# Prologue of a two-layer expert kernel: order of two loads, idle products among the logits, and who normalises the rows

## The reference, cut to what matters

```python
x = x + 0.5 * ffn(layernorm(x), Wg, W11, W12, W2)
x = x + attn(layernorm(x), ...)
x = x + 0.5 * ffn(layernorm(x), Wg, W11, W12, W2)

def ffn(x, Wg, W11, W12, W2):          # 8 experts, 2 chosen per row
    scores, idx = top_k(softmax(x @ Wg), 2)
    scores = scores / (scores.sum() + 1e-8)
    gate, value = x @ W11[e], x @ W12[e]          # 256 -> 512
    return sum over the two e of scores[e] * ((gate * sigmoid(gate) * value) @ W2[e])
```

## Time and profile before

| | us |
|---|---|
| median of 3 runs | 987.4 |
| lowest and highest | 986.29, 987.94 |
| the profiled execution, its own time | 985.32 |
| its span | 983.5 |
| busy in the span: PE, DVE, ACT, POOL | 903.3, 582.7, 391.2, 575.8 |
| mean granted clock, as a share of 2.4 GHz | 0.962 |

### The profile page before, as it was taken

One profiled execution on the slowest core, in us unless ns is written; L12 is line 12 of the kernel. 1 busy time (PEld: TensorE's weight loads), 2 busy tenths in 40 slices (PEclk: granted clock), 3 DMA queues, 4 the chain that ended last, 5 costly groups with the idle time before them and its releaser, 6 DMA issues.

```text
span 983.5 us, 19046 instructions
## 1 busy us (share of the span) xinstructions
PE 903.3 (92%) x5396; PEld 778.3 (79%) x5399; DVE 582.7 (59%) x1394; ACT 391.2 (40%) x768; POOL 575.8 (59%) x605
## 2 busy tenths in 40 slices
PE   7769999999999999949897996899999999999994
PEld 6658888888888888827775874688888888888883
DVE  3986565675665655556726887555555555555551
ACT  3644244343443433325443775133333333333331
POOL 3435565666666665357514651577777777777762
PEclk9979999999999999968999996899999999999997
DMA  9654525526336281086202555654433333333332
GB/s 313 204 179 138 205 69 189 185 75 205 131 126 203 94 267 56 28 267 193 65 1 85 162 179 176 214 139 77 78 55 75 54 74 75 53 75 53 54 46 25
DMA packets 83936, 121.50 MB, mean 124 GB/s; under 512 B 12944, under 2 KB 62736, under 8 KB 83888
## 3 DMA queue, kind: packets, MB, share of 16 engines
q1 hardware_dynamic: 45376, 57.88, 18.1%
q0 software_dynamic: 24992, 37.32, 17.5%
q10 hardware_dynamic: 13520, 25.70, 7.7%
HBM read 73.62 MB, written 47.25 MB: 123 GB/s over the span
## 4 chain that ended last, share of the span: by engine, by line
PE 76%; DVE 7%; DMA 5%; ACT 5%; POOL 3%; issue 3%; ACTq 1%; SPq 0%; POOLq 0%
PE bank L1456 40%; PE bank L1479 20%; PE bank L1465 6%; PE bank L1448 3%; PE bank L1577 3%; ACT work L879 1%; DMA seq<-xt 1%; PE bank L1635 1%; DMA seq<-x_rows 1%; PE bank L1625 1%; ACT work L812 1%; ACT work L870 1%; DMA out_rows<-yb,idx_i 1%; PE bank L1394 1%; DMA seq<-y_rows 1%
## 5 line engine op out<-in xcount | busy, mean ns | idle before, releaser
L1165 DVE TENSOR_TENSOR sg<-sg,bank 128x512 f32<-128x512 f32 x142 | 97.7, 688 | 282.7 <-ACT sg L741 282.7
L1456 PE MATMUL bank<-w_hi,xt_hi 128*128 x568 | 237.8, 419 | 4.5 <-DVE xt_lo L1154 4.4
L1456 PE MATMUL bank<-w_hi,xt_lo 128*128 x568 | 225.1, 396 | 0.0
L1456 PE MATMUL bank<-w_lo,xt_hi 128*128 x568 | 225.0, 396 | 0.0
L733 ACT ACTIVATE yb<-bank,gates_in 128x256 f32<-128x256 f32 x142 | 67.3, 474 | 313.8 <-PE bank L1479 276.0
L551 POOL DMA_INDIRECT xg<-xn_rows,idx_i x142 | 140.1, 987 | 72.6 <-issue 41.4
L555 POOL DMA_INDIRECT gates_in<-gate_rows,idx_g x142 | 136.2, 959 | 48.0 <-issue 42.7
L1479 PE MATMUL bank<-w_hi,ft_hi 128*128 x568 | 160.3, 282 | 2.2 <-ACT yb L733 2.2
L1479 PE MATMUL bank<-w_lo,ft_hi 128*128 x568 | 160.5, 283 | 0.0
L1479 PE MATMUL bank<-w_hi,ft_lo 128*128 x568 | 160.4, 282 | 0.0
L565 POOL DMA_INDIRECT out_rows<-yb,idx_i x71 | 114.9, 1619 | 63.2 <-ACT yb L733 53.4
(11 more groups left out here) (289 smaller groups left out, 1293.8 us busy)
## 6 DMA issues: line engine op xcount, KB each, us to landing
w_lo<-w_lo_rows SPq DMA_DIRECT2D x32, 512.0 KB, 4.6
w_lo_rows<-w_lo ACTq DMA_DIRECT2D x16, 512.0 KB
xn_rows<-work SPq DMA_DIRECT2D x14, 512.0 KB, 3.4
seq<-y_rows SPq DMA_DIRECT2D x10, 512.0 KB, 5.2
x_all<-x SPq DMA_DIRECT2D x8, 512.0 KB, 9.0
w_lo_rows<-in_sb ACTq DMA_DIRECT2D x16, 256.0 KB, 2.4
gate<-x SPq DMA_DIRECT2D x16, 256.0 KB, 5.8
seq<-w ACTq DMA_DIRECT2D x7, 512.0 KB, 4.5
```

What stands on the lines that cost most here:

```text
L1165: nc.vector.tensor_tensor(sg[p], sg[p], ps_g[p][:], ALU.mult).then_inc(f_step, 1)
L1456: last = nc.tensor.matmul(dst[p][:], xt[p][:, c, :], of(w), start=(c == 0 and n == 0), stop=(c == DC - 1 and n == len(parts) - 1))
```

## The change

Four things, all in the prologue.

- SyncE asks for five parts of `xt` first, and then for x and the rest of `xt` in turn.
- TensorE gets eight idle products ahead of the loop over the chunks, and four ahead of each chunk's logits. They write bank 3, which `fold` uses later.
- `apply_x` leaves VectorE. GpSimd does it for chunks 0, 2, 4 and 6, each behind that chunk's `rsqrt_x`, with the same waits, that for the zero rows among them.
- ScalarE does it for chunks 1, 3, 5 and 7: three after the variances of chunks 2, 4 and 6, the last where `apply_x(7)` was. The waits of SyncE, ScalarE and VectorE for these rows follow (`norm_dve` becomes `norm_pool`).

```diff
--- before.py
+++ after.py
@@ -270,7 +270,7 @@
         xn_x_out = [sem(f"xn_x_out{b}") for b in range(3)]
         y_in = [sem(f"y_in{b}") for b in range(3)]
         y_out = [sem(f"y_out{b}") for b in range(2)]
-        x_early, x_late, half_sum, summed, norm_dve, norm_act, r_ready = (sem(n) for n in ("x_early", "x_late", "half_sum", "summed", "norm_dve", "norm_act", "r_ready"))
+        x_early, x_late, half_sum, summed, norm_pool, norm_act, r_ready = (sem(n) for n in ("x_early", "x_late", "half_sum", "summed", "norm_pool", "norm_act", "r_ready"))
         x_in = [sem(f"x_in{b}") for b in range(4)]
         x_out = [sem(f"x_out{b}") for b in range(4)]
         xn_out = [sem(f"xn_out{b}") for b in range(2)]
@@ -317,9 +317,11 @@
                 sp.dma_start(x_all[:, k * G:(k + 1) * G, :], rows(x, k)).then_inc(x_all_in[k], 16)
 
             sp.dma_start(wg_sb[:, :, 0:E], wg.rearrange("(c p) e -> p c e", p=P)).then_inc(s_wg, 16)
-            for k in range(NCH):
-                sp.dma_start(xt_raw[0][:, k * CH:(k + 1) * CH], xt[0:P, k * CH:(k + 1) * CH]).then_inc(xt_in[k], 16)
-                load_x(k)
+            for k in range(NCH + 4):
+                if k < NCH:
+                    sp.dma_start(xt_raw[0][:, k * CH:(k + 1) * CH], xt[0:P, k * CH:(k + 1) * CH]).then_inc(xt_in[k], 16)
+                if k >= 4:
+                    load_x(k - 4)
             sp.dma_start(pw_sb, pw.rearrange("(c p) d -> p c d", p=P)).then_inc(s_setw, 16)
             sp.dma_start(wint_sb, wint.rearrange("(c p) n -> p c n", p=P)).then_inc(s_setw, 16)
             sp.dma_start(woutt_sb, woutt).then_inc(s_setw, 16)
@@ -333,10 +335,7 @@
                     e = expert_of_slot(sp, 0)
                     load_up(sp, 0, e)
                     load_down(sp, e)
-                if k < NCH // 2:
-                    sp.wait_ge(norm_dve, k + 1)
-                else:
-                    sp.wait_ge(norm_act, k + 1 - NCH // 2)
+                sp.wait_ge(norm_act if k % 2 else norm_pool, k // 2 + 1)
                 sp.dma_start(rows(xn_dram, k), xn_x[k % 3]).then_inc(xn_x_out[k % 3], 16)
 
             def store_gates(r):
@@ -593,8 +592,21 @@
                 for t in range(ET - 3, ET):
                     scatter(t)
 
+            def apply_x(k):
+
+                pool.wait_ge(rstd_ready, k + 1)
+                if k == 2:
+                    pool.wait_ge(pads_out, 32)
+                if k >= 3:
+                    pool.wait_ge(xn_x_out[k % 3], 16 * (k // 3))
+                for t in range(k * G, (k + 1) * G):
+                    last = nc.gpsimd.tensor_scalar(xn_x[k % 3][:, t % G, :], x_all[:, t, :], x1_rstd[:, t:t + 1], x1_mean[:, t:t + 1], ALU.mult, ALU.add)
+                last.then_inc(norm_pool, 1)
+
             for k in range(NCH):
                 rsqrt_x(k, k % 2)
+                if k % 2 == 0:
+                    apply_x(k)
             experts(0)
 
             def sum_choices(i):
@@ -708,7 +720,7 @@
                     if n == 0:
                         apply_x(NCH - 1)
                     if n == NQB - 1:
-                        act.wait_ge(norm_dve, NCH // 2)
+                        act.wait_ge(norm_pool, NCH // 2)
                     if n > 0:
                         (high_up, high_value, high_down)[n - 1](0)
 
@@ -782,7 +794,7 @@
 
             for k in range(NCH):
                 variance_x(k)
-                if k > NCH // 2:
+                if k % 2 == 0 and k > 0:
                     apply_x(k - 1)
             tiles_by_p(0)
             router_exp(0)
@@ -949,17 +961,6 @@
                     last = nc.vector.bn_aggr(mv[:, b, t, :], bnst[:, b, t, :])
                 last.then_inc(mv_ready, 1)
 
-            def apply_x(k):
-
-                dve.wait_ge(rstd_ready, k + 1)
-                if k == 2:
-                    dve.wait_ge(pads_out, 32)
-                if k >= 3:
-                    dve.wait_ge(xn_x_out[k % 3], 16 * (k // 3))
-                for t in range(k * G, (k + 1) * G):
-                    last = nc.vector.tensor_scalar(xn_x[k % 3][:, t % G, :], x_all[:, t, :], x1_rstd[:, t:t + 1], x1_mean[:, t:t + 1], ALU.mult, ALU.add)
-                last.then_inc(norm_dve, 1)
-
             link, at = chain(route_step, 0)
 
             def top2_of(r, k):
@@ -1033,6 +1034,7 @@
                 if r == 0:
                     row_of = idx_s
                     dve.wait_ge(norm_act, NCH // 2)
+                    dve.wait_ge(norm_pool, NCH // 2)
                     link(nc.vector.scalar_tensor_tensor(idx_s, token, -1.0, pad, ALU.add, ALU.add))
                     nc.vector.tensor_scalar(idx_i[:], idx_s, L - 1, None, ALU.bitwise_and).then_inc(slots_ready, 1)
                 else:
@@ -1208,8 +1210,6 @@
                 top2_of(0, k)
                 if k % 2 == 1:
                     sum_chosen(0, k // 2)
-                if 3 <= k < 7:
-                    apply_x(k - 3)
                 if k in (3, 5, 7):
                     places_of(0, (k - 3) // 2)
             router_of(0)
@@ -1532,7 +1532,9 @@
             pe.wait_ge(const_ready, 1)
             center()
             pe.wait_ge(wg_ready, 1)
+            keep_busy(bank[3][:], before.unsqueeze(1).to_broadcast([P, G, P]), 8)
             for k in range(NCH):
+                keep_busy(bank[3][:], before.unsqueeze(1).to_broadcast([P, G, P]), 4)
                 logits_x(k)
                 if k > 0:
                     ranks_of(0, k - 1)
```

## The result

| | before | changed |
|---|---|---|
| median of 20 runs each, side by side, us | 986.93 | 989.8 |
| lowest and highest, us | 983.63 to 988.38 | 985.26 to 992.1 |
| profiled execution, time and span, us | 985.32, 983.5 | 991.35, 989.6 |

The ratio is 1.0026, 95% interval 1.0014 to 1.0038: slower, by 2.6 us on 987.4. The profiled execution of before lies 1.6 us under its median and that of the change 1.5 us over its own, so the two profiles show a larger difference (6.0 us) than the medians. The 20 executions of the change fall into two groups, 7 from 985.3 to 987.5 us and 13 from 989.5 to 992.1, with none between; those of before have no such gap. The median of the change is the low edge of its slower group, and its profile is of that group.

What follows compares the result with a forecast made beforehand. The prologue's end, on DVE some 2.5 us behind PE, was taken as the bound. PE's idle products at a mostly slow clock move DVE's loop end from 44.98 to 49.2: 987.4 + 4.2 = 991.6 us, range 983 to 996.

Steps and rivals of the forecast that it cites:

- the fast level lost: Prologue logits: PE drops from 2.4 to 1.2 GHz after early chunks and DVE waits for it; +4.2 us, chance 0.48.
- How many chunks are fast: Prologue logits on PE: three chunks at the fast level, five at the slow; one more or less is 2.5 us.
- The forecast end of the loop: DVE's prologue loop: ends at 49.2 us against 44.98 before, +4.2.
- Twelve products ahead: Idle products before PE's first logits: eight at 0.42 and four at 0.23, 4.3 us, bounds 2.8 and 5.0.
- A chunk at either level: PE's logits of a chunk with four idle products: 2.8 us at 2.4 GHz, 5.3 at 1.2 GHz.
- From the last logits to the end of the loop: DVE behind PE's last logits: choice of experts 1.86, `sum_chosen` 0.38 and `places_of` 2.31, 4.55 us.
- The loads: Prologue loads: first x block lands at 13 to 16 us, delaying ScalarE's first variance at no cost; zero rows at 30.4.
- Rival 3: Prologue loads: transposed x comes no sooner, hidden by PE's idle products; less than 1 us, no chance of its own.
- The side chain: GpSimd and ScalarE in the prologue: waits for zero rows and roots covered by PE's late logits, costing nothing.
- rival 1: Prologue: fast level holds and the chain through GpSimd and ScalarE bounds; -4.0, 983.4 us, chance 0.28.
- rival 2: Prologue: fast level holds, side chain bounds and DVE holds GpSimd up; +1.8, 989.2 us, chance 0.24.
- The hold-ups: GpSimd slowed beside DVE's `places_of` and `router_of`: 2 x 1.2 and 3.4, 5.8 us in all, within rival 2.

Runs made afterwards that it cites:

- run 2: The kernel before with only the 40 idle products added; ratio 1.0051 to the kernel before.
- run 7: The change with eight idle products ahead of each chunk instead of four; ratio 0.9969 to the kernel before.
- run 11: The change itself, unaltered, timed once more for its profile; ratio 1.0024 to the kernel before, median 990.47 us, profiled execution 985.98.
- run 4: The kernel before with only the order of the loads changed; ratio 0.9978 to the kernel before.
- run 10: The kernel before with the change's order of loads and the zero rows asked for early; ratio 0.9970 to the kernel before.
- run 9: The change, idle products kept, with the two stores of zero rows asked for early; ratio 1.0030 to the kernel before.
- run 1: The change without any of its 40 idle products; ratio 0.9994 to the kernel before.
- run 3: The kernel before with only the normalised rows moved from VectorE to GpSimd and ScalarE; ratio 1.0000 to the kernel before.
- run 5: The change without idle products, zero rows asked for behind x of chunk 3; 981.53 against 987.86 us for the kernel before, ratio 0.9941.
- run 12: The change with early zero rows and six idle products per chunk instead of four; 982.84 us, ratio 0.9953 to the kernel before.
- run 6: Run 5 with GpSimd taking the root of chunk k+1 ahead of its block of chunk k; ratio 0.9952 to the kernel before.
- run 8: The change with the eight idle products ahead of the loop alone, none between chunks; ratio 0.9996 to the kernel before.

## Why the prediction was right, point by point

- **Direction and mechanism.** 991.6 was forecast, +4.2; measured are 989.8 and +2.6, inside the range. The case called "the fast level lost" happened: early chunks fast, the rest slow, DVE waiting for PE. Run 2 pins the loss on the products and run 7 on the level. That the median came within 2 us of the forecast owes something to luck: none of the four profiled executions with this mixture had three fast chunks, and the median stands at the edge between two groups of executions, one level with the kernel before and one 3 to 5 us above it.
- **How many chunks are fast.** Three were forecast. One execution had one and part of a second, another had four with the last partly slow. The step failed as a single figure: the number varies between executions, and most of 6.2 us of prologue (73.46 - 67.26) hangs on it; 0.8 of that is the twelve products ahead, 5.09 against 4.28. The forecast end of the loop, 49.2, lies between the two draws, 52.54 and 46.73.
- **Twelve products ahead.** Forecast 4.3 us within 2.8 to 5.0; measured 5.09 and, in run 11, 4.28. The first is just above the upper bound: in that profile all twelve were slow.
- **A chunk at either level.** Forecast 2.8 and 5.3; measured 2.74, and (44.58 - 18.74) / 5 = 5.17.
- **From the last logits to the end of the loop.** Forecast 4.55; measured 52.54 - 47.83 = 4.7, and from there to `xt_lo` 20.9 against 20.5 before.
- **The loads.** First variance forecast for 13 to 16, measured 15.69; zero rows forecast for 30.4, the block behind them started at 30.44. Rival 3's price, less than 1 us because the idle products hide the order, is borne out for the case that came: run 2, with the old order, ends its prologue within 0.3 us of the change. Without idle products the order is worth 2 us (runs 4 and 10).
- **The side chain.** Slack in the change, as forecast (run 9). With PE out of the way (runs 1 and 7) the end was not -4.0 (rival 1) nor +1.8 (rival 2) but +0.1 and +0.2. The hold-ups that I had put at 5.8 us are there in kind: blocks of 3.23 and 4.08 instead of 2.2, a step of 1.07 instead of 0.24. But they are not what decides. In runs 3 and 7 GpSimd's blocks of chunks 2 and 6 take 2.2 to 2.4 us, hardly held up, and the prologue still ends 0.95 and 0.17 late: with block 2 starting behind the zero rows at 31.20 and 30.52 the chain is late by its start. In run 5 the wait is gone and the last block falls into a gap of DVE. In run 12 the wait is gone and the last two blocks take 3.22 and 3.12 all the same, so hold-ups don't always go with it.
- **The Trainium skill.** In SBUF — State Buffer, SBUF: two separate sides, a DVE operation with two SBUF inputs and one of GpSimd exclude each other. Runs 1 and 6 agree in so far as either side takes longer beside the other (3.23 and 4.08 against 2.2; 0.99 against 0.75); that the loser stands still for the whole of the other's instruction is not shown by them. TensorE: Matmul & The Clock Gate, Part 1 says that the number of slow products at a start differs from run to run; the two profiles of the change agree (twelve products in 5.09 and in 4.28 us), and I should have given the level a spread from it.

What stays open: of the 7.96 us by which the prologue ends later in the profile, 6.0 are left in the execution's time. The traces show where the rest comes back: at the last L1465 of the first expert stage the two kernels are 7.34 apart (412.92 and 420.26), at the middle stage's first L1625 (now L1627) 5.98 (519.81 and 525.79), so mostly behind the first expert stage; why is open. Run 7 is 3 us below the kernel before by its median though its prologue ends level. At the same two places it is 0.81 and 2.58 ahead of before, so it gains there too; its profiled execution ends only 1.0 below that of before, and the cause is not shown.

## What to carry to other kernels

Filler on an engine is paid in series whenever the engine has no gaps: price it at the slow level, and take it in only if the fast level is shown to last in every execution, since here four per chunk cost some 3 us against none at all and nearly 6 against eight. When work leaves the engine that bounds a stage, follow its new owner's waits to the end of the stage first: here the 4.3 us by which VectorE's loop ended earlier without idle products were all gone at the end of the prologue (run 1), and asking earlier for the two small stores of zero rows brought 4.5 us there (run 5). Take two profiles of a kernel whose clock changes in mid-stage before reading a size off one, and see whether its times fall into groups before trusting their median.

## What was not expected of the hardware

- **The moment of the fall moves.** The same program lost the 2.4 GHz level at 14.6 us in one execution and at 19.7 in another, with TensorE busy all the time from 7 us to well behind the fall in both; the time at the end of the prologue differs by 6.2 us.
- **The column of the granted clock starts at 1.00.** The prediction had set it aside for the durations; the idle products confirm that. Eight of them in 3.50 us at 6.41 (run 8) and twelve in 5.09 are at some 0.42 each, the slow level, while the column reads 1.00. From its first fall on the durations agree with it; ahead of that they decide:

```profile
6.41 3.50 PE L1366 MATMUL bank<-before 128*128 128x512 bf16 x8 [0.42 <-DVE wg_sb L1206]
```

```profile
6.00:8.00 2.00, 1.59 (x4) 0.59 (x5) 0.45 (x5) 1.58 (x3) 0.00 (x0) 1.00 1.00 365
```

- **The hold-up goes both ways.** DVE's L1005, 1.22 us alone, took 1.47 beside GpSimd's block (run 8), and its L1097 0.99 instead of 0.75 (run 6).
